# A graph layer on 8192 nodes: the row stripes that are read a second time come in another order

## What is computed

```python
def ref(x, adj, W):                       # x 8192 x 128, adj 8192 x 8192, W 128 x 128, all float32
    h = maximum(layernorm(x), 0)
    A_hat = adj + eye(8192)
    d = sum(A_hat, axis=1) ** -0.5
    A_norm = d[:, None] * A_hat * d[None, :]
    return x + relu(A_norm @ (h @ W.T))
```

## Time and profile before

| | us |
|---|---|
| three runs, median (lowest to highest) | 1311.45 (1303.54 to 1344.44) |
| profiled execution, its own time | 1313.91 |
| span of the profile, first to last instruction | 1312.3 |
| busy in the span: PE, DVE, ACT, POOL | 990.0, 843.1, 531.3, 52.6 |
| mean granted clock of TensorE | 0.888 of full |
| moved by DMA | 377.11 MB, 287 GB/s over the span |

### The profile page before, as it was taken

How to read it: one execution, slowest core, us unless ns; L and a number is a source line. 1 busy time by engine, 2 the same in 40 slices (tenths; PEclk the granted TensorE clock), 3 DMA queues, 4 the chain that set the end, 5 groups by cost and what they waited for, 6 DMA issues and landing times.

```text
span 1312.3 us, 8882 instructions
## 1 busy us (share of the span) xinstructions
PE 990.0 (75%) x2363; PEld 452.2 (34%) x2363; DVE 843.1 (64%) x958; ACT 531.3 (40%) x1596; POOL 52.6 (4%) x61
## 2 busy tenths in 40 slices
PE   1542454576687756796969898999987898998896
PEld 1431121232233322342424343444433343443342
DVE  5443144366576655786868887888864665776675
ACT  2885665575474462735354535555010000000001
POOL 4000000000000000000000000000000000000001
PEclk9876686678789887997989998999999899999998
DMA  9999999999999999999999999999699999999992
GB/s 305 308 368 341 335 354 335 298 329 351 353 338 296 301 305 237 315 274 281 270 254 271 237 247 298 272 296 247 165 324 289 236 306 300 266 281 279 270 290 71
DMA packets 289857, 377.11 MB, mean 287 GB/s; under 512 B 11152, under 2 KB 269328, under 8 KB 289808
## 3 DMA queue, kind: packets, MB, share of 16 engines
q1 hardware_dynamic: 154192, 192.51, 54.1%
q10 hardware_dynamic: 135616, 184.04, 49.6%
HBM read 372.31 MB, written 4.19 MB: 287 GB/s over the span
## 4 chain that ended last, share of the span: by engine, by line
DMA 38%; PE 35%; ACT 9%; ACTq 9%; DVE 4%; issue 3%; SPq 2%; POOLq 0%; POOL 0%; DVEq 0%
PE bank L452 34%; DMA slot<-in_adj_dram 33%; ACT junk L507 7%; ACTq L295 5%; DMA thirds<-in_adj_dram 3%; DVE adjT L649 3%; ACTq L289 2%; DMA support<-in_x_dram 1%; SPq L250 1%; ACTq L258 1%; ACTq L250 1%; ACT acc L482 1%; ACT slot L496 1%; SPq L313 1%; SPq L321 1%
## 5 line engine op out<-in xcount | busy, mean ns | idle before, releaser
L452 PE MATMUL bank<-adjT,support 128*128 128x512 f32 x2048 | 944.8, 623 | 223.7 <-DVE adjT L649 223.7
L452 PEld LDWEIGHTS bank<-adjT,support 128*128 128x128 f32 x2048 | 405.6, 201 | 741.4 <-issue 734.5
L649 DVE STREAM_TRANSPOSE adjT<-slot 128x1024 f32<-128x1024 f32 x380 | 460.0, 1231 | 278.8 <-DMA slot<-in_adj_dram 190.9
L507 ACT ACTIVATE junk<-slot 128x384 bf16<-128x384 f32 (+2 forms) x495 | 233.4, 473 | 275.2 <-issue 129.1
L496 ACT ACTIVATE slot<-slot 128x6144 f32<-128x6144 f32 (+11 forms) x56 | 166.2, 2969 | 92.1 <-DMA slot<-in_adj_dram 60.4
L525 ACT ACTIVATE near<-near,dinv 128x128 f32<-128x128 f32 x64 | 20.4, 390 | 365.5 <-DVE near L736 315.0
L649 DVE STREAM_TRANSPOSE adjT<-thirds 128x1024 f32<-128x1024 f32 x70 | 84.1, 1228 | 44.9 <-DMA thirds<-in_adj_dram 33.0
L649 DVE STREAM_TRANSPOSE adjT<-near 128x1024 f32<-128x1024 f32 x62 | 76.6, 1239 | 34.6 <-PE bank L452 34.6
L507 ACT ACTIVATION_READ_ACCUMULATOR junk<-slot 128x1 f32 x495 | 92.3, 187 | 0.0
L634 DVE TENSOR_REDUCE part<-slot 128x5 f32<-128x1920 f32 (+2 forms) x45 | 85.0, 1890 | 0.0
L507 ACT ACTIVATE junk<-near 128x256 bf16<-128x256 f32 (+1 forms) x176 | 69.3, 395 | 18.0 <-issue 12.6
(11 more groups left out here) (54 smaller groups left out, 178.2 us busy)
## 6 DMA issues: line engine op xcount, KB each, us to landing
slot<-in_adj_dram SPq DMA_DIRECT2D x100, 768.0 KB, 15.1
slot<-in_adj_dram ACTq DMA_DIRECT2D x100, 768.0 KB, 14.9
slot<-in_adj_dram SPq DMA_DIRECT2D x48, 512.0 KB, 13.4
slot<-in_adj_dram ACTq DMA_DIRECT2D x48, 512.0 KB, 13.0
near<-in_adj_dram SPq DMA_DIRECT2D x30, 512.0 KB, 16.0
near<-in_adj_dram ACTq DMA_DIRECT2D x30, 512.0 KB, 17.1
slot<-in_adj_dram ACTq DMA_DIRECT2D x8, 1536.0 KB, 14.8
slot<-in_adj_dram SPq DMA_DIRECT2D x8, 1536.0 KB, 15.4
```

The lines of the kernel that those rows point to most:

```text
L452: ins = nc.tensor.matmul(bank[g % BANKS][:], support[:, v * R + t, :], adjT[at % TURNS][:, r, :], start=(n == first_of[g] and t == 0), sto ...
L507: nc.scalar.activation(junk[at % JUNKS][:, :n], cells[:, c, :], ACT.Copy, accum_out=part[u % 2][:, k, c:c + 1]).then_inc(junk_done, 1)
L649: nc.vector.transpose(adjT[at % TURNS][:].rearrange("p t (c i) -> p t c i", i=Q), half.rearrange("p c (t r) -> p t c r", r=Q)).then_inc(t_ ...
```

## The change

The stripes of the re-read come in the order 0, 12, 11, 10, ..., 1, where it was 0, 1, 2, ..., 12. The loads (`landing`), the cells (`rest`), the banks (`group`) and the finals all follow that list. Which cells are read again, how a stripe is cut into pieces, the buffers' turns, the sizes and the first pass are as they were.

```diff
+    FAR_ROWS = NB - 1 - BAND
+    AGAIN_ROWS = [0] + list(reversed(range(1, FAR_ROWS)))
...
-    for u in range(NB):
+    for u in AGAIN_ROWS:
         again[u] = []
...
-    rest = [(u, v, m) for u in range(NB) for m in again[u] for v in range(landing[m][2], landing[m][2] + landing[m][3])]
+    rest = [(u, v, m) for u in AGAIN_ROWS for m in again[u] for v in range(landing[m][2], landing[m][2] + landing[m][3])]
...
-        return u if v <= u + BAND else NB + u
+        return u if v <= u + BAND else NB + AGAIN_ROWS.index(u)
...
-    finals = [u for u in range(FAR_ROWS, NB)] + list(range(FAR_ROWS))
+    finals = [u for u in range(FAR_ROWS, NB)] + AGAIN_ROWS
...
-        return last_of[finals[n] if n < NB - FAR_ROWS else NB + finals[n]]
+        return last_of[finals[n] if n < NB - FAR_ROWS else FAR_ROWS + n]
```

More of the change, by code:

```diff
@@ L128, in gnn_kernel @@
     place = {(u, v): n for n, (u, v, m) in enumerate(order)}
-    FAR_ROWS = NB - 1 - BAND
     def group(u, v):
-        return u if v <= u + BAND else NB + u
+        return u if v <= u + BAND else NB + AGAIN_ROWS.index(u)
     first_of, last_of = {}, {}
@@ L723, in finish @@
                 else:
-                    dve.wait_ge(used, transposed(last_of[NB + u]))
+                    dve.wait_ge(used, transposed(last_final(n)))
                     dve.wait_ge(kept_acc, u + 1)
                     for cc in range(R):
-                        ins = nc.vector.tensor_tensor(to[:, cc], by_tile(bank[(NB + u) % BANKS])[:, cc],
+                        ins = nc.vector.tensor_tensor(to[:, cc], by_tile(bank[(FAR_ROWS + n) % BANKS])[:, cc],
                                                       by_tile(acc[:, u, :])[:, cc], ALU.add)
```

## The result

| | before | with the change |
|---|---|---|
| median of six runs each, us | 1310.56 (1295.84 to 1344.44) | 1327.99 (1321.0 to 1351.29) |
| profiled execution, us | 1313.91 | 1325.52 |
| its span, us | 1312.3 | 1323.9 |
| mean granted clock of TensorE | 0.888 | 0.885 |

The ratio is 1.0187, with a 95% interval from 1.0116 to 1.0258. The change makes the kernel slower by 1 to 3%. The forecast was 1317 us and no measurable difference, the range 1300 to 1338; the time is that of the second rival, 1329 us.

A forecast was written before the change was run, and what follows sets the result against it. DMA never slack in the re-read, with PE held up by adj late on SP's queue. Product's end 1308.5 plus tail 9.5 made a span of 1318.0; plus 1.6 minus 2.5 gave 1317 us, range 1300 to 1338.

The forecast's parts named there:

- the second rival: SP's queue, carrying adj and all finals, bounds the re-read from 983.9 us to the last piece: 1329 us, chance 0.22.
- What bounds the kernel: Re-read: DMA never slack, PE at 3.43 us a cell, DVE waiting 58.3 us for adj, late on SP's queue.
- (a): Tail after the last product: one final left instead of four combines, 9.5 us instead of 14.4, gain 4.9.
- (b): Narrow rows, cells 178 to 213: finals delay SP's adj loads, waits sum to 44.7 us, loss about 14 us.
- prices of 2.85 and 8.55 us: SP's queue beside ACT's adj traffic: half a cell of adj takes 2.85 us, one final 8.55 us.
- (c): Wide rows at the end: 30 cells at 3.84 us, 115.2, and the last 12 at 3.43, 41.2 us.
- My walk: Narrow rows from cell 178: SP's queue followed piece by piece at set prices, with DVE at 3.43 us a cell.
- The signs: Re-read and tail: three long adj waits between cells 181 and 206, near 205 GB/s beside them, tail 9 to 10 us.
- SP's queue never rests: Re-read: hardly any final gets the cheap price, so SP's queue is the bound; 1329 us, chance 0.22 for 1323 to 1345.
- Bytes are all that counts: Re-read: same DMA bytes, so waits only change places and the tail's gain stays; 1306.5 us, chance 0.24.
- Finals get cheap: Narrow rows: ACT's queue runs dry, finals cost 3.7 to 5 us and adj 2.55; 1280 us, chance 0.06.
- DVE's waits for a combine: Finals 4 to 7: a combine waits for an addition and its reload behind a store; under 5 us, within the forecast.

The follow-up runs named there:

- e1: New order with each final's stores and reloads of x divided between SP's and ACT's queues; median 1278.8 us, ratio 0.9653 to the kernel before.
- e4: Old order with the stores of finals 0 to 13 and the reloads for finals 2 to 15 left out; 1279.11 us, ratio 0.9823 to the kernel before.
- e10: Old order, all on SP, with 24 more 64 KB loads of x behind the reloads following finals 3 to 8; median 1352.58 us, re-read 375.2 us.
- e2: Old order with each final's stores and reloads of x divided between SP's and ACT's queues; median 1284.87 us, ratio 0.9732 to the kernel before.

## Why the prediction was right and where it was off

The mechanism was right: SP's queue, held up by finals, makes its halves of adj late. The time fell into the range, but its centre missed: no measurable difference was forecast (0.4%), and the interval of the ratio, 1.0116 to 1.0258, excludes that. The measured time is the number of a rival that had a chance of 0.22. The re-read lost 25.1 us where the forecast had 10.6, and in the profiled span 8.3 us of that are hidden by a first pass that was shorter by chance. Step by step, with times of the changed kernel moved by 8.3 us so that both re-reads begin at 928.38:

- **What bounds the kernel.** Right: the late halves of adj take turns with PE. Where no queue has all finals PE alone is the bound (e1 to e4). The change moves the waits for adj from 58.3 to 73.1 us.
- **(a) The tail.** Forecast 9.5 us, measured 9.1; gain 4.9 against 5.3.
- **(b) The narrow rows.** Forecast waits of 15.4, 11.8, 2.3, 2.8, 10.3 and 2.1 us; measured, in that order, 14.97, 10.22, 4.35, 2.08, 11.26 and 1.47, and two more of 3.48 and 2.89. Cell 214 was forecast for 1152.1 without a wait of its own. PE was through with the cell before it at 1148.38 (1137.84 + 10.54), moved 1156.7: 4.6 late, so the loss against before's 1138 is 19 us, forecast 14. The prices of 2.85 and 8.55 us did well here, with some luck. DVE's waits in these rows, 50.7 us, left PE idle for only 36.6. What had been put at nothing filled that up: 8 turned-back finals (3.5 us) and slower matmuls behind the waits (some 7 us; granted clock 0.92 from 1029 to 1173, where it was 1.00 before).
- **(c) The wide rows: the term that was mis-sized.** Forecast 115.2 + 41.2 = 156.4 us for the 42 cells from 214 on. Measured 1314.82 - 1148.38 = 166.4, 10.0 more; with the 4.6 of (b) that is the 14.6 by which the product's end was off (1323.1 moved, forecast 1308.5). The first 30 cells took about 120.6 us, 4.02 a cell. The 3.84 of before had been read from 31 cells that begin just behind its longest wait, so that wait isn't in it, and it didn't carry over. The last 12 cells took about 45.9 us, forecast 41.2. Waits of 8.60, 7.70 and 4.58 us stand in (c), the last of them among the 12 cells that I had taken as free. My walk stopped at cell 213, where its own queue, with a final and three half cells to come (17.1 us), had the next piece late by some 5 us. SP then had less waiting of its own than before (71.4 against 99.6 us over the same stretch), so it came to the wide rows with less in hand. That last is a guess from the rows, not an experiment.
- **The signs.** Right: three long waits between cells 181 and 206, each behind a load that SP issued 17, 13 and 17 us after ACT's half of the same piece; a sum over 60 us; a tail of 9.1 us that waits for no x. Wrong: some 205 GB/s beside the waits. It was 313 in the one that ends at 1056.66, and 210 came behind it. Wrong too: DMA full until 10 to 15 us before the product's end (its share is 0.78 from 1290 to 1295 and 0.02 from 1295 to 1300, so some 20 us), and nearly no wait over the last 12 cells (4.58).
- **The rivals.** "SP's queue never rests" gave 1329 us, product's end 1320.3; measured 1327.99 and 1323.1. The number is right, and of the picture the main line: SP's queue moved data in each stretch of 2 us from 975 to 1295 (so it had before, until 1287), while ACT's moved next to nothing (under 0.02 MB) in 24 of these stretches, 48 us, up to 1277 (34 us before, none in e1 up to 1223). But its ledger by count is contradicted by e10, and its own condition, waits of over 55 us in (b), wasn't met (50.7). "Bytes are all that counts" is refuted by e1: the same bytes at 344 and at 265 GB/s. The rule of the Trainium skill that went with it ("DMA: Bandwidth & Descriptors", section "Issuing engines are not separate DMA queues"), that DMAs started on several engines save only the time to start them, doesn't hold here. "Finals get cheap" didn't happen. DVE's waits for a combine were small: one of 4.16 us for POOL stands in DVE's timeline of the changed kernel, none of that size behind cell 178.
- **Not seen.** Dividing the finals between the queues. By the prediction's own prices half a final on each queue costs 4.3 us on both, so each queue has 91 x 2.85 + 14 x 4.3 = some 320 us of work, less than the 333.4 that PE needs. The gain could have been forecast; whether a divided final costs less than 4.3 us on each queue e1 and e2 don't show, as PE is the bound there. Why a final costs a queue three times its bytes is read, not tested: the packets of the profile bear out the turns that the prediction names, but no run changes the length of the rows.

## What to carry to other kernels

Where a piece of data comes in halves over two queues, count what else each queue carries: the later half sets the time, and small DMAs in only one of them cost far more than their bytes. Divide such traffic as the data is divided. With that the new order came out 3.5% and the old one 2.7% below the kernel before, where the order by itself had cost 2%; with divided queues only the shorter tail of the new order was left of it. And compare the stage that was changed before the totals: builds whose first pass is the same program differed there by up to 47 us.

## What the runs showed of the hardware

- Two queues with adj moved 368 GB/s, one alone 205. DMA's busy share was 1.06 in the first and 1.11 in the second, so the share doesn't tell them apart; the GB/s do.
- With work on both queues they moved equal numbers of packets, 1481 and 1452 in 12 us, at 1.80 and 2.18 MB; the queue with the shorter rows got fewer bytes.
- The same traffic of 64 KB DMAs (rows of 512 bytes) made the re-read 62.3 us longer in one queue and about 1 us when divided between two, where PE was the bound (394.7, 333.4 and 332.4 us).
- The first passes of 14 profiles ended between 916 and 963 us with unchanged instructions.
